# A two-step graph layer on one core: another end of each VectorE group, layer 0 written straight into SBUF, and the diffusion tiles placed anew around the attention pairs

## The reference

```
h = relu(layernorm(x));  x = x + quantised_gnn(h, adj)             # layer 0
X = relu(layernorm(x));  R = (adj + I) / row_sums                  # layer 1
for s in 0, 1:
    logits = X_a W1 W2 (X_a W3)^T                                  # 2048 x 2048
    A   = softmax over each row's top-p set, p = 0.9               # threshold per row
    X_f = R X_f                                                    # "diffusion"
    X_a = A X_a                                                    # "attention"
    Z  += X_f U1[s] + X_a U2[s]
x = x + layernorm(X + Z) * gamma + beta
```

## Time and profile before

| | |
|---|---|
| median of 3 runs | 1532.36 us (1529.28 to 1532.55) |
| the profiled execution's own time | 1530.33 us |
| its span | 1528.5 us |
| PE busy | 1253.8 us, 82% |
| DVE busy | 1141.0 us, 75% |
| ACT busy | 603.1 us, 39% |
| POOL busy | 272.3 us, 18% |
| mean granted PE clock | 0.947 |

### The profile page before, as it was taken

How to read it: one execution, slowest core, us unless ns; L and a number is a source line. 1 busy time by engine, 2 the same in 40 slices (tenths; PEclk the granted TensorE clock), 3 DMA queues, 4 the chain that set the end, 5 groups by cost and what they waited for, 6 DMA issues and landing times.

```text
span 1528.5 us, 18985 instructions
## 1 busy us (share of the span) xinstructions
PE 1253.8 (82%) x6522; PEld 617.6 (40%) x6522; DVE 1141.0 (75%) x1972; ACT 603.1 (39%) x1137; POOL 272.3 (18%) x231
## 2 busy tenths in 40 slices
PE   0458999994898699899899996699799369999995
PEld 0224555541343354445455552244344134445442
DVE  7976566653998998898798302897798999589456
ACT  1323444437611544554532435800444054443231
POOL 3212343330132020211221200010010001011011
PEclk9889999998999799999999999799899789999998
DMA  6224655647143011211201005343111102122235
GB/s 213 82 93 164 229 210 205 240 162 271 55 137 135 11 63 37 75 44 40 97 28 56 36 23 196 133 137 124 49 57 36 67 21 70 42 70 69 99 118 184
DMA packets 62069, 159.64 MB, mean 104 GB/s; under 512 B 5856, under 2 KB 5856, under 8 KB 57632
## 3 DMA queue, kind: packets, MB, share of 16 engines
q1 hardware_dynamic: 61984, 158.64, 29.5%
HBM read 99.11 MB, written 59.51 MB: 104 GB/s over the span
## 4 chain that ended last, share of the span: by engine, by line
PE 45%; DVE 26%; issue 14%; ACT 6%; DMA 3%; POOL 3%; SPq 1%; DVEq 1%; POOLq 0%; ACTq 0%
PE AB L738 13%; PE AB L741 6%; DVE WS L1208 6%; PE UB L606 5%; PE RB L706 5%; PE AB L596 4%; PE TB L615 3%; DVE turns L1164 3%; DMA AD<-z_d 2%; PE RB L708 2%; ACT squares L923 2%; PE XB L606 1%; POOL RT L503 1%; DVE E L1364 1%; DVE w L1393 1%
## 5 line engine op out<-in xcount | busy, mean ns | idle before, releaser
L1208 DVE SCALAR_TENSOR_TENSOR WS<-E,g 128x2048 bf16<-128x2048 f32 x146 | 348.4, 2437 | 3.0 <-issue 1.7
L738 PE MATMUL AB<-XR,turns 128*128 128x512 f16 x1024 | 244.5, 382 | 0.0
L706 PE MATMUL RB<-VR,turns 128*128 128x512 f16 x1024 | 234.5, 379 | 0.0
L1293 DVE TENSOR_REDUCE g<-E 128x1 f32<-128x2048 f32 x32 | 72.9, 2278 | 110.8 <-ACT E L916 110.4
L706 PEld LDWEIGHTS RB<-VR,turns 128*128 128x128 f16 x1024 | 100.0, 98 | 111.3 <-issue 0.6
L738 PEld LDWEIGHTS AB<-XR,turns 128*128 128x128 f16 x1024 | 101.0, 99 | 108.6 <-issue 4.9
L741 PE MATMUL AB<-XR,turns 128*128 128x512 f16 x512 | 131.4, 379 | 0.0
L978 ACT ACTIVATE turns<-TB 128x512 f16<-128x512 f32 x128 | 75.3, 594 | 130.6 <-PE TB L621 130.5
L503 POOL TENSOR_TENSOR RT<-RT,AD 128x512 f32<-128x512 f32 x32 | 56.6, 1768 | 350.6 <-ACT RT L958 350.6
L708 PE MATMUL RB<-VR,turns 128*128 128x512 f16 x512 | 117.7, 379 | 0.0
L606 PE MATMUL UB<-UW,XT 128*128 128x512 f16 x384 | 88.2, 379 | 27.9 <-ACT XT L867 27.7
(11 more groups left out here) (253 smaller groups left out, 1965.1 us busy)
## 6 DMA issues: line engine op xcount, KB each, us to landing
turns<-adj_parts SPq DMA_DIRECT2D x64, 512.0 KB, 3.7
E<-adjT SPq DMA_DIRECT2D x16, 1024.0 KB, 5.9
adj_parts<-turns SPq DMA_DIRECT2D x16, 1024.0 KB, 6.4
x_parts<-XHL SPq DMA_DIRECT2D x32, 256.0 KB, 3.0
v_parts<-VHL SPq DMA_DIRECT2D x32, 256.0 KB, 2.0
VR<-v_parts SPq DMA_DIRECT2D x2, 4096.0 KB, 13.8
XR<-x_parts SPq DMA_DIRECT2D x2, 4096.0 KB, 24.2
z_d<-UO SPq DMA_DIRECT2D x31, 256.0 KB, 2.0
```

Of the source, the lines that this page charges most:

```text
L706: i = mm(RB[:, :], AT[:, 0, j, :], VR[:, j, k % 2, :], start=False, stop=False)
L738: mm(AB[:, :], ET[:, 0, j, :], XR[:, j, y_, :], start=(j == 0 and y_ == 0), stop=False)
L1208: return v.scalar_tensor_tensor(junk[t % 2], e, g4[:, k, t:t + 1], e, op, ALU.mult, accum_out=g4[:, F_, t:t + 1])
L1293: ct(v.tensor_reduce(row(A2)[:, t:t + 1], E[:, slot, :], AX.X, ALU.max))
```

## The change

- `first_guess` takes the square root on VectorE: a guess from the bits and one Newton step that gives twice the root (so Z_P / 2 below). The wait for POOL is gone.
- `settle` masks the first tile ahead of the register load (with a row of thresholds that is 0 where a flag is set), masks the other three in the branch, and takes the four reciprocals together at the end, with a semaphore of their own (`s_rden`).
- A flagged tile now goes through `in_order`, with a constant `order` (the numbers 1 to 2048 in fp16, built on POOL at the start in 1 + 11 instructions in the place of gamma and beta, which are loaded in the last group). `rank_equals` is left for rows whose ties reach the eighth value of the window; these go through `bisect` first.
- Layer 0 writes XR and VR directly. The stores to x_parts and v_parts and both reloads before step 0 are gone. VR for step 1 is loaded ahead of the last group of step 0 (`v_in`), XR after the first diffusion tile's AD (`x_in`).
- 1 diffusion tile (`r_tile`) between the logits of group 0 and 1, 8 in the loop, one in front of each of groups 0, 1, 2, and two in the pairs of groups 0 and 1 each. None is left in the pairs of group 2.

```diff
-R_GROUPS = 3
-R_BEHIND = 2
+R_GROUPS = 2
+R_BEHIND = 3
 R_FIRST = T - R_GROUPS * (G // 2) - R_BEHIND
...
+        def step_order(s, logits, terms, r_tile, r_tiles, pairs, r_behind):
             logits(s, 0)
             terms(s, 0)
+            r_tile(s)
             logits(s, 1)
             r_tiles(s)
             for g in range(NG):
                 if g + 1 < NG:
                     terms(s, g + 1)
-                if 1 <= g <= R_BEHIND:
-                    r_behind(s, r_of(g, 0) - 1)
+                if g < R_BEHIND:
+                    r_behind(s, R_FIRST + g * (1 + G // 2))
                 pairs(s, g)
...
             def pairs(s, g):
                 last = s == 1 and g == NG - 1
+                if s == 0 and g == NG - 1:
+                    v_in()
+                    at_hi_in(1, 0)
+                    at_lo_in(1, 0)
                 if last:
+                    sp.wait_ge(s_kept, 2 * T)
+                    sp.dma_start(bet, beta.partition_broadcast(P)).then_inc(s_gb, 16)
+                    sp.dma_start(gam, gamma.partition_broadcast(P)).then_inc(s_gb, 16)
...
+            q.memset(order[:, 0:1], 1.0).then_inc(s_order, 1)
+            for k in range(LOG_N):
+                pool.wait_ge(s_order, k + 1)
+                q.tensor_scalar(order[:, 2 ** k:2 ** (k + 1)], order[:, 0:2 ** k], 2.0 ** k, None,
+                                ALU.add).then_inc(s_order, 1)
...
-                q.tensor_tensor(g4[:, SIG, :], g4[:, VAR, :], powc[:, 1, 0:G], ALU.pow).then_inc(s_gsig, 1)
...
+                    ct(v.tensor_scalar(row(SIG).bitcast(I32), row(VAR).bitcast(I32), 0.5, ROOT, ALU.mult, ALU.add))
+                    ct(v.reciprocal(row(A2), row(SIG)))
+                    ct(v.tensor_tensor(row(A2), row(A2), row(VAR), ALU.mult))
+                    ct(v.tensor_tensor(row(SIG), row(SIG), row(A2), ALU.add))
...
+            def in_order(e, t):
+
+                v.scalar_tensor_tensor(WS[:, :], e, g4[:, THR, t:t + 1], order, ALU.is_equal, ALU.mult)
                 v.drain()
+                v.max(h8[:, t, :], WS[:, :])
                 v.drain()
+                v.scalar_tensor_tensor(h8[:, t, :], order[:, 0:WIN], g4[:, BAD, t:t + 1], h8[:, t, :], ALU.is_ge, ALU.mult)
+                v.drain()
+                v.tensor_reduce(row(A1)[:, t:t + 1], h8[:, t, :], AX.X, ALU.max)
+                v.drain()
+                v.scalar_tensor_tensor(e, WS[:, :], row(A1)[:, t:t + 1], e, ALU.is_le, ALU.mult)
+                v.drain()
...
+                ct(v.tensor_tensor(row(A1), row(A1), h8[:, :, WIN - 1], ALU.max))
                 ct(v.scalar_tensor_tensor(row(A1), row(BAD), 1.5, row(A1), ALU.is_gt, ALU.mult))
...
+                masked(tiles[0][0], 0, SAFE)
...
                         with dve.If(dve.value_load(total[0:1, 1 + t:2 + t].bitcast(I32)) != NEVER):
                             bisect(E[:, slot, :], t)
+                            rank_equals(E[:, slot, :], t)
+                            v.memset(g4[:, BAD, t:t + 1], 1.0)
+                            v.drain()
                         with dve.If(dve.value_load(total[0:1, 5 + t:6 + t].bitcast(I32)) != NEVER):
-                            rank_equals(E[:, slot, :], t)
-                        keep(slot, t)
+                            in_order(E[:, slot, :], t)
+                        masked(slot, t, THR).then_inc(s_kept, 1)
                 with dve.If(any_flag == NEVER):
-                    for slot, t in tiles:
-                        keep(slot, t)
+                    v.drain()
+                    dve.sem_inc(s_kept, 1)
+                    for slot, t in tiles[1:]:
+                        masked(slot, t, THR).then_inc(s_kept, 1)
+                dve.wait_ge(s_kept, G * gq + G)
+                ct(v.reciprocal(row(A1), row(DEN)))
+                v.tensor_scalar(rden[:, sl], row(A1), 1.0 / SE, None, ALU.mult).then_inc(s_rden, 1)
```

198 lines of the change are left out of this document (107 added, 91 removed).

## The result

The changed kernel takes **1469.61 us** (median of 4 runs, 1468.06 to 1473.25) against 1531.43 for the kernel before beside it (4 runs, 1529.28 to 1532.55): a ratio of 0.9602, 95% interval 0.9582 to 0.9622. The profiled execution took 1471.02 by its own time, its span is 1469.2: 59.3 less than before, where the sum had 48.8 less.

What follows compares the result with a forecast made beforehand. The prediction took the steps to be PE's, with holes where it waits for ACT and, in step 1's group 1, late VectorE. Terms 3 - 6.8 - 29 - 16.0 = -48.8 took 1530.3 to 1481 us, range 1465 to 1499.

Steps and rivals of the forecast that it cites:

- Start, +3: Kernel start: 12 small POOL instructions delay its pow and VectorE's next work; 0 to 4.6 us, taken as +3.
- Layer 0, 0: Layer 0: the removed stores and reloads are not waited for by PE or VectorE in the chain, so 0.
- Step 0's head, +2.7: Start of step 0: two more diffusion tiles mostly fill PE's holes; group 0's subtraction at 510.6 against 507.90, +2.7 us.
- The other number for the head, +4.8: Start of step 0: if VectorE holds out POOL's sum, each moved tile may pay 2.1 us more on ACT: +4.8.
- Group 1 of step 0, 0: Step 0's second group: groups 0 and 1 keep their pairs, so 0.
- Group 2 of step 0, -9.5: Step 0's third group: four half tiles fewer save 14.0 us, but PE waits 4.5 for VectorE: -9.5.
- Step 1 up to group 1's first tile, -29: Step 1's first part: `in_order` takes 7.7 us in place of 22.0 on two flagged tiles; -29, swallowing the head's +2.6.
- Group 2 of step 1, -16.0: Step 1's third group: the half tiles' cost of 16.0 us goes, with VectorE 5 ahead: -16.0.
- 1 (flagged tiles as dear): Step 1's group 1: the two flagged tiles get no shorter and PE's wait stays near 30; 1508 us, chance 0.07.
- 4 (`bisect`): Flagged tiles: a tied eighth value sends one tile to `bisect`, 181 us while PE waits; 1676 us, chance 0.05.
- Rival 2: Step heads: moved tiles are paid back through POOL's sum in ACT's queue or late data; 1493 to 1505 us, chance 0.13.
- Rival 3: Whole kernel quicker: PE keeps its clock, the first mask hides wholly, POOL's build hides; 1469 us, chance 0.13.

Runs made afterwards that it cites:

- run 8: Changed kernel with layer 0's stores of the x and v halves and the two 4 MB reloads before step 0 put back: 1481.74 us, ratio 0.9682 to the kernel before.
- run 4: Changed kernel with the diffusion tiles in their old places (none between the logits, halves in the pairs of groups 0, 1 and 2): 1493.56 us, ratio 0.9763.
- run 5: Changed kernel with each step's first diffusion tile put behind the second group's logits again: 1494.1 us, ratio 0.9758 to the kernel before.
- run 7: Changed kernel with the square root of a group's variance as a pow on POOL again: 1477.26 us, ratio 0.9654 to the kernel before.
- run 2: Changed kernel with the first tile's mask back inside the branch, not speculatively ahead of it: 1474.62 us, ratio 0.9648 to the kernel before.
- run 3: Changed kernel with `rank_equals` in place of `in_order` for the flagged tiles: 1498.61 us, ratio 0.9799 to the kernel before.
- run 6: Changed kernel with the tile in front of group 0 written ahead of group 1's terms on every engine, PE's order unchanged: 1488.97 us, ratio 0.972.

## Why the prediction was right, and where it was off

The places of the gain and the mechanisms of the large terms held, and the range held the time. The sum was 10.5 us too small (48.8 for 59.3): 4.9 in group 2 of step 0, 2.3 in its group 1, 2.0 in layer 0, 1.9 in step 0's head, 1.1 in group 2 of step 1, less 1.4 at the start and 0.3 in group 3 of step 0. Term by term:

- **Start, +3: measured +4.4** on VectorE's and PE's chain (47.23 against 42.81, and 42.83 with the ramp built later), and still 4.4 at layer 0's first product. The upper bound of the prediction, 4.6, was the right one: the eleven instructions take 8.33, near its 8.6 and far from the 1.2 of its lower bound.
- **Layer 0, 0: measured -2.0** from its first product to the logits (254.3 against 256.2). This isn't shown to be the change: the changed kernels lie between 250.7 and 254.3, the one with the stores put back lowest of all, and there is one trace of before. But the reload, costed at nothing, is worth 12.4 once tile 0 stands in the first hole (run 8). The prediction did say that its data must be there; it gave no price for the case that they aren't.
- **Step 0's head, +2.7: measured +2.5 at group 0's subtraction** (157.5 after the first logits against 155.0). That the number fits is in part luck. The first hole ends 3.6 later and not 2 (ACT's 3.0 as forecast, and 1.0 for the clock at the first logits, where the prediction took 1 off), and the step from the second moved tile to the subtraction is 3.5 and not 5.6, since the sum on POOL that stands in it took 1.27 and not the 3.37 of the earlier trace rows. The tiles alone cost 4.8 (run 4), and the other edits give 2.3: VectorE's first threshold of group 1 comes that much sooner. By the end of group 0 it is +0.8: the pairs run 1.7 shorter, with PE's granted clock at 1.00 in the 22 us behind the subtraction and 0.90 before. The prediction took 1 off for the clock ahead of the subtraction and nothing behind it.
- **The other number for the head, +4.8:** POOL's sum took 1.56 and 1.27 on the two moved tiles of step 0, so nothing was paid here; in runs 5 and 8 the last one took over 3 and PE's wait at the subtraction grew from 1.45 to 3.5. By the Trainium skill ("SBUF — State Buffer", Who interferes with whom) a VectorE instruction with two SBUF inputs contends with a GpSimd one that reads SBUF. The rows of runs 5 and 8 and of the changed kernel agree; the moment at which the two meet decides whether the 2.1 us are paid.
- **Group 1 of step 0, 0: measured -2.3**, not foreseen. 1.1 is POOL's sum in front of the group, 2.28 in place of 3.37, with PE's wait 2.49 in place of 3.54; run 7 gives it back. 1.2 is clock: PE ran at 1.2 GHz for 3 us behind that wait and for over 6 before (granted 0.93 and 0.85 in 23 us), and the rest of the group took the same 94.8 in both.
- **Group 2 of step 0, -9.5: measured -14.4. This is the term that was mis-sized.** The -14.0 for the halves was right (run 4: 13.3). The +4.5 for "PE waits 4.5" on VectorE was 0.3. Counted from group 1's end, VectorE had the first tile of group 3 ready at 103.2 before; the forecast's 842 is 101.7, and it was 839.68 - 741.21 = 98.5. Of the 4.8 between before and changed, 2.5 are the mask with the branch behind it, which had been given "0 to 2.35" of gain and lies wholly beside the branch (run 2; without it PE waits 2.82 and group 3 is 3.6 longer). 1.1 is the pow's (ACT takes the first threshold 3.9 us after group 1's end, 5.0 before: the "only about 1 us" of the prediction). The remaining 1.2 lies in the search and in `settle`, where VectorE's instructions that are stretched beside POOL's are other ones (before, one more pass of 3.24 in place of 2.35 and small ones of 1.11 and 1.15; now a small one of 1.14); the reciprocals stand behind the masks and have no part in it. Both ends of "840.2 to 842.5" were stated and 842 was taken: in the time of before it came at 838.7, ahead of both.
- **Step 1 up to group 1's first tile, -29: measured -28.9** (by the table head +1.7 and group 1 -30.7). `in_order` at 7.8 and 7.7 was costed at 7.7. Run 3 gives 28.2 of it to `rank_equals` alone.
- **Group 2 of step 1, -16.0: measured -17.1**; run 4 has 15.5 for the halves, and 1 or more is the root's (run 7: 3.5).

Of the rivals, 1 (flagged tiles as dear) fell with run 3, 4 (`bisect`) with the count of 144. Rival 2 (tiles paid back) falls by run 4, but its two mechanisms can be made to happen: run 6 shows ACT's order (18.1), run 8 the late data (12.4). Rival 3 (quicker, 1469) met the time, though only in part by its own terms: the mask does hide wholly and the clock gave a little (mean granted 0.947 before, 0.971 after, by the runs' listing), but POOL's build, which it took as hidden, is not, and the 2.3 of group 1 and the 2.0 of layer 0 stand in no forecast; so its number is in part luck.

## What to carry to other kernels

A block of work fills a hole on PE only if the other engines' queues take their part of it in the right order and its data are there: tile 0 in step 0's first hole was worth 12 us (run 5), and nothing with a reload ahead of it (run 8); the tile in front of group 0 cost 10.0 and 8.7 more, with PE's order unchanged, once ACT's exponentials stood behind it (run 6). So price a moved block by what covers what: each tile in front of a group covers ACT's 8 us of exponentials, the loop's eighth tile covers step 0's second hole, which is VectorE's late threshold, and where nothing is covered (step 1's head) it costs its full length, which is where the last 2.3 us came from. When several covers end within a few us of each other, price an edit by the whole chain and not by its slack: after this change a delay of 1 us on VectorE or POOL shows in the cells (run 7).
